# Six rounds of a local attention layer: a hardware loop over one body, or six bodies in sequence

## The chip, the cores and the metric

The kernel runs on one core of a Trainium2 chip (trn2). The metric is the device time of one execution in microseconds, as the median of several runs. Each core has five engines with instruction streams of their own: TensorE (PE), VectorE (DVE), ScalarE (ACT), GpSimd (POOL) and the sync engine (SP). They meet only at semaphores.

## What is computed

The reference is a network of four blocks on an activation of 4 x 512 tokens of 128 channels. Each block computes `x = x + s * silu(g)` from two sub-networks. The change is in the second sub-network of block 1, a transformer of six layers with attention in a window of 32 tokens:

```python
for i in range(6):
    x = attn_layer(shift_tokens(x), Wqkv[i], q_scale[i], k_scale[i], Wo[i]) + x
    x = ffn_layer(shift_tokens(x), ln_g[i], ln_b[i], W1[i], b1[i], W2[i], b2[i]) + x
```

`attn_layer` has 16 heads of 64: l2-normalised q and k, rotary factors, softmax over the token's own window of 32 and the one before, and the output product. `ffn_layer` is a layer norm, a gated product of 2 x 341 columns with an exact gelu, and the product back. All layers have the same shapes; only the weights differ. All data is float32.

## The kernel before

The activation lies in on-chip memory with channels on partitions and 2048 tokens along the free axis, in one of 20 slabs. The program is a sequence of phases. `phase` (lines 49 to 63) allocates semaphores, opens a block in which each engine gets its own list of instructions, and ends with clearing each semaphore (line 62, the clears dealt out to the five engines in turn) and an all-engine barrier (line 63). The block has a closing synchronisation of its own, which the profile puts down to line 58.

`local_transformer` (line 481) first has a phase that loads the attention weights of layer 0, the rotary tables and the masks, builds the shifted copy of the activation, and ends on VectorE with the product of tables and scales (line 518). Then it runs the layers as a hardware loop:

```python
with nc.Fori(0, F1_LAYERS) as layer:
    local_layer(nc, m, ins, layer, w, ...)
```

`local_layer` (line 536) is one phase with 48 semaphores. It has 32 units (16 tiles of 128 tokens, two halves of the heads), which pass through the engines as a pipeline written out by hand, unit i of one step beside units i-1 to i-6 of others (lines 747 to 799 on TensorE, 879 to 918 on ScalarE, 1019 to 1067 on VectorE, 1087 to 1091 on GpSimd). `project` (line 617) makes q and k of a unit with the products of line 623; a float32 product of 128x512 shows as two passes in the profile, so that a unit has four. `square` (line 807), `sum_squares` (937), `normalise` (949) and `rope` (1085, 957) follow. After the units the forward part runs in 12 chunks (lines 734, 735, 744). On the sync engine a round begins with the transfer of this layer's forward weights (`F1F`, line 598), goes on with the moves of the values, and ends with the transfer of the next layer's attention weights (`F1A`, line 612), which VectorE uses in line 1066. VectorE's last work in a round is `finish(3)`: the addition of line 1013 and two copies of line 1017. ScalarE begins a round with a table load (line 878) and has a second one in its middle (line 905).

After the layers comes a phase with one Silu on ScalarE (line 533), then the recurrent network, which has a hardware loop of its own with two rounds (line 1127) that stays as it is.

Of the kernel before, what the change touches and what calls it, by code (L numbers as in the profile page):

```python
# [26 lines left out]
def offsets(parts):  # L27

    at, where = 0, {}
    for name, width in parts:  # L30
        where[name] = (at, width)
        at += width
    return where, at
# [14 lines left out]
@contextmanager  # L48
def phase(nc, names, raised=False):

    with ExitStack() as ctx:
        sems = [ctx.enter_context(nc.semaphore(n)) for n in names.split()]
        if raised:
            for s in sems:
                nc.sync.sem_inc(s, RAISED)
            nc.all_engine_barrier()
        with nc.Block(no_gpsimd_drain=True) as block:  # L58
            yield (block, *sems)
        engines = [nc.sync, nc.tensor, nc.vector, nc.scalar, nc.gpsimd]  # L60
        for n, s in enumerate(sems):
            engines[n % len(engines)].sem_clear(s)
        nc.all_engine_barrier()  # L63
# [404 lines left out]
F1_LAYERS = 6  # L468
# [12 lines left out]
def local_transformer(nc, m, ins, xn, g_out):  # L481

    where, width = offsets(F1_ATTENTION + F1_FORWARD)
    W = m.slab(2, 3)[:, 0:width]
    for_attention = W[:, 0:offsets(F1_ATTENTION)[1]]
    for_forward = W[:, offsets(F1_ATTENTION)[1]:width]
    angles = m.slab(5)[:, 0:1024].rearrange("p (t k d) -> p t k d", t=4, k=4)
    tables = m.slab(5)[:, 1024:2048].rearrange("p (t k d) -> p t k d", t=4, k=4)
    shifted = m.slab(6, 2)[:, 0:BATCH * STRIP].rearrange("p (b t) -> p b t", b=BATCH)
    qBD = m.slab(7)[:, 256:1280].rearrange("p (n w h q) -> p n w h q", n=PAIRS, w=2, h=2)  # L490
    hA = m.slab(8, 2)[:, 0:BATCH * PADSEQ].rearrange("p (b t) -> p b t", b=BATCH)
    hB = m.slab(10, 2)[:, 0:BATCH * PADSEQ].rearrange("p (b t) -> p b t", b=BATCH)

    def w(name, a=0, n=None, rows=P):
        o, width = where[name]
        return W[0:rows, o + a:o + (a + n if n else width)]

    with phase(nc, "tables_loaded copied") as (block, tables_loaded, copied):
        @block.sync
        def _(sp):  # L500
            sp.dma_start(for_attention, ins["F1A"][F1_LAYERS - 1]).then_inc(tables_loaded, 16)
            sp.dma_start(m.slab(5)[:, 0:1024], ins["rotary"]).then_inc(tables_loaded, 16)
            sp.dma_start(m.masks[:, 0:2 * KEYS], ins["masks"]).then_inc(tables_loaded, 16)
            sp.wait_ge(tables_loaded, 48)

        @block.vector
        def _(dve):
            by_batch = xn.rearrange("p (b t) -> p b t", b=BATCH)
            nc.vector.memset(hB[:, :, 0:1], 0.0)
            nc.vector.memset(hA[:, :, 0:1], 0.0).then_inc(copied, 1)  # L510
            nc.vector.tensor_copy(hA[:, :, 1:PADSEQ], by_batch).then_inc(copied, 1)
            dve.wait_ge(copied, 2)
            for b in range(BATCH):
                for half, start in ((slice(0, 64), 1), (slice(64, P), 0)):
                    nc.vector.tensor_copy(shifted[half, b, REACH:STRIP], hA[half, b, start:start + SEQ])
            dve.wait_ge(tables_loaded, 48)
            by_side = w("scales").rearrange("p (o n) -> p o n", o=1).broadcast_to([P, 4, 4 * HD1])
            nc.vector.tensor_tensor(tables.rearrange("p t k d -> p t (k d)"), angles.rearrange("p t k d -> p t (k d)"), by_side, ALU.mult)

        @block.gpsimd  # L520
        def _(pool):
            nc.gpsimd.memset(m.weights[:, 0:2 * PAIRS * STRIP].rearrange("p (c t) -> p c t", c=2 * PAIRS)[:, :, 0:REACH], 0.0)
            nc.gpsimd.memset(shifted[:, :, 0:REACH], 0.0)
            nc.gpsimd.memset(m.slab(7)[:, 256:1280], 0.0)
            nc.gpsimd.memset(m.slab(16, 2), 0.0)

    with nc.Fori(0, F1_LAYERS) as layer:
        local_layer(nc, m, ins, layer, w, for_attention, for_forward, angles, tables, shifted, qBD, hA, hB)

    with phase(nc, "silu_done") as (block, silu_done):  # L530
        @block.scalar
        def _(act):
            nc.scalar.activation(g_out.rearrange("p (b t) -> p b t", b=BATCH), hA[:, :, 1:PADSEQ], ACT.Silu)

def local_layer(nc, m, ins, layer, w, for_attention, for_forward, angles, tables, shifted, qBD, hA, hB):
# [41 lines left out]
    def place(u):  # L578
        tile, half = u // 2, u % 2
        return tile // 4, tile % 4, half  # L580

    def moves(u):
        return 16 * sum(2 if place(n)[1] == 0 else 3 for n in range(u % 4, u + 1, 4))

    with phase(nc, "forward_loaded qk_product qT_product kT_product v_product score_product pT_product pv_product out_product "
# [9 lines left out]

        @block.sync
        def _(sp):
            sp.dma_start(for_forward, ins["F1F"][bass.ds(layer, 1)].rearrange("l p n -> (l p) n")).then_inc(forward_loaded, 16)
            for u in range(UNITS):
                b, t, half = place(u)  # L600
                sp.wait_ge(v_copied, u + 1)
                if u >= 4:
                    sp.wait_ge(pv_product, u - 3)
                sp.dma_start(v[u % 4][:, 1, :], tile_v[u % 4][REACH:P, :]).then_inc(moved[u % 4], 16)
                sp.dma_start(v[u % 4][REACH:KEYS, 0, :], tile_v[u % 4][0:WINDOW, :]).then_inc(moved[u % 4], 16)
                if t:
                    sp.dma_start(v[u % 4][0:REACH, 0, :], tile_v[(u - 2) % 4][P - REACH:P, :]).then_inc(moved[u % 4], 16)
            for n in range(4):
                sp.wait_ge(moved[n], moves(UNITS - 4 + n))
            sp.wait_ge(forward_loaded, 16)  # L610
            sp.wait_ge(out_product, UNITS // 2)
            sp.dma_start(for_attention, ins["F1A"][bass.ds(layer, 1)].rearrange("l p n -> (l p) n")).then_inc(next_loaded, 16)
            sp.wait_ge(next_loaded, 16)

        @block.tensor
# [1794 lines left out]
def block1(nc, m, ins, x):  # L2410
    xn = m.slab(1)
    spread_norm(nc, m, x, xn, tag="l1ln", refine=False)
    g, s = m.slab(2), m.slab(4)
    local_transformer(nc, m, ins, xn, g)
    recurrent_network(nc, m, ins, xn, s)
    add_product(nc, x, s, g)
# [220 lines left out]
```

## Time and profile before

| | us |
|---|---|
| median of 3 runs | 5192.08 |
| the runs | 5191.89, 5192.08, 5202.68 |
| the profiled execution | 5195.5 |
| its span, first to last instruction | 5193.7 |
| mean granted TensorE clock | 0.806 |
| busy: PE, DVE, ACT, POOL | 3971.8, 3768.7, 2570.9, 2171.7 |
| first round begins, last round ends (after the span's start) | 223.1, 2511.3 |

Times in rows are microseconds from the start of the span. In the timeline a row gives the start, the busy time of the merged instructions, the engine, the line, the operation, what it writes and reads with its shape, how many were merged, and in brackets how long the engine had been idle and what released it.
### The profile page before, as it was taken

What the parts mean: (1) busy time and instruction counts of PE and PEld (TensorE: products, weight loads), DVE (VectorE), ACT (ScalarE), POOL (GpSimd) and SP (SyncE); (2) the same over time, 40 slices, a digit from 0 to 9 for tenths busy, and PEclk for the clock granted to TensorE, in tenths of its full rate; (3) what the DMA queues carried; (4) which work ended last, traced back from release to release, by engine and by line L of the source; (5) the groups of instructions that cost most, each with busy time, mean ns of one, the idle gap of its engine ahead of it and who ended that gap; (6) DMA issues with size and microseconds to landing.
All of it is one profiled execution on the core that took longest, in us unless ns stands there. A gap on an engine that the chain in (4) does not pass through costs nothing. (4 is left out here: it accounts for less than half of the span.)

```text
span 5193.7 us, 75861 instructions
## 1 busy us (share of the span) xinstructions
PE 3971.8 (76%) x25476; PEld 2536.7 (49%) x25476; DVE 3768.7 (73%) x7356; ACT 2570.9 (50%) x6832; POOL 2171.7 (42%) x1600
## 2 busy tenths in 40 slices
PE   5389799799799799799777767956666666588897
PEld 2166466466466466466343343433333333355564
DVE  5799599599599598698354544399999999832343
ACT  2188488488488488488222121233333333326343
POOL 0177277277276376376120310066666666500000
PEclk8699899899899899899777687855555555567898
DMA  0011111111111111111000000000000000000000
GB/s 17 28 41 42 38 42 42 37 42 42 37 41 41 39 40 42 37 42 43 28 1 9 1 25 1 0 1 1 1 1 1 1 1 1 1 7 1 22 1 9
DMA packets 48634, 109.67 MB, mean 21 GB/s; under 512 B 8944, under 2 KB 9200, under 8 KB 46704
## 3 DMA queue, kind: packets, MB, share of 16 engines
q1 hardware_dynamic: 48240, 104.66, 6.6%
q8 instruction: 217, 3.56, 0.3%
q14 instruction: 177, 1.45, 0.1%
HBM read 31.23 MB, written 1.05 MB: 6 GB/s over the span
## 5 line engine op out<-in xcount | busy, mean ns | idle before, releaser
L1085 POOL TENSOR_TENSOR slabs<-slabs 128x512 f32<-128x512 f32 x768 | 975.4, 1300 | 368.7 <-DVE slabs L949 368.7
L1782 DVE MAX8 slabs<-slabs 128x8 f32<-128x512 f32 x1084 | 691.6, 679 | 57.4 <-ACT slabs L1719 57.4
L1808 POOL TENSOR_SCALAR slabs<-slabs 128x512 f32<-128x512 f32 x256 | 400.3, 1564 | 470.4 <-DVE slabs L1788 470.4
L1074 POOL TENSOR_TENSOR slabs<-slabs 128x768 f32<-128x768 f32 x192 | 341.9, 1781 | 567.9 <-DVE slabs L926 567.9
L623 PE MATMUL psum<-slabs 128*128 128x512 f32 x768 | 413.2, 665 | 214.7 <-DVE slabs L949 149.5
L1703 ACT ACTIVATE slabs<-slabs 128x512 f32<-128x512 f32 x316 | 211.6, 719 | 727.8 <-DVE slabs L1788 727.8
L854 ACT ACTIVATE slabs<-slabs 128x96 f32<-128x96 f32 x1536 | 551.4, 360 | 37.2 <-PE psum L667 35.7
L1641 PE MATMUL psum<-constants,slabs 128*128 128x128 f32 x1264 | 305.5, 407 | 299.7 <-POOL slabs L1811 299.3
L1784 DVE MATCH_REPLACE8 slabs<-slabs 128x512 f32<-128x512 f32 x768 | 513.0, 675 | 0.0
L1632 PE MATMUL psum<-slabs 8*128 8x512 f32 (+1 forms) x632 | 346.5, 1087 | 164.2 <-ACT slabs L1719 164.1
L659 PEld LDWEIGHTS psum<-weights,slabs 128*128 128x128 f32 x3072 | 372.2, 192 | 101.3 <-issue 86.1
L1641 PEld LDWEIGHTS psum<-constants,slabs 128*128 128x128 f32 x1264 | 222.6, 208 | 383.7 <-POOL slabs L1811 343.6
L957 DVE TENSOR_TENSOR slabs<-slabs 128x512 f32<-128x512 f32 x384 | 388.4, 1012 | 8.8 <-POOL slabs L1085 7.4
L659 PE MATMUL psum<-weights,slabs 128*128 128x96 f32 x3072 | 370.0, 274 | 8.8 <-ACT weights L826 8.8
L1811 POOL TENSOR_TENSOR slabs<-slabs 128x512 f32<-128x512 f32 x256 | 325.2, 1270 | 21.4
L623 PEld LDWEIGHTS psum<-slabs 128*128 128x128 f32 x768 | 141.2, 205 | 359.7 <-DVE slabs L949 185.3
L937 DVE TENSOR_REDUCE slabs<-slabs 128x16 f32<-128x1024 f32 x192 | 231.9, 1208 | 113.8 <-ACT slabs L807 112.9
L242 POOL TENSOR_TENSOR slabs<-slabs 128x512 f32<-128x512 f32 x12 | 17.4, 1484 | 671.2 <-POOLq L63 671.2
L854 ACT ACTIVATION_READ_ACCUMULATOR slabs<-slabs 128x1 f32 x1536 | 286.7, 187 | 0.0
L667 PE MATMUL psum<-constants,slabs 128*96 128x128 f32 x1536 | 244.9, 283 | 42.4 <-ACT slabs L847 39.2
L679 PEld LDWEIGHTS psum<-slabs 96*64 96x64 f32 x6144 | 195.7, 138 | 143.3 <-issue 134.8
L1632 PEld LDWEIGHTS psum<-slabs 8*128 8x128 f32 (+1 forms) x632 | 113.2, 294 | 300.9 <-ACT slabs L1719 281.4
(392 smaller groups left out, 8378.0 us busy)
## 6 DMA issues: line engine op xcount, KB each, us to landing
slabs<-slabs SPq DMA_DIRECT2D x192, 192.0 KB, 2.5
slabs<-slabs SPq DMA_DIRECT2D x192, 128.0 KB, 2.5
slabs<-F1A SPq DMA_DIRECT2D x7, 2176.0 KB, 8.4
slabs<-slabs SPq DMA_DIRECT2D x144, 64.0 KB, 2.1
slabs<-F1F SPq DMA_DIRECT2D x6, 580.5 KB, 4.2
slabs<-S SPq DMA_DIRECT2D x4, 645.0 KB, 6.5
weights<-M SPq DMA_DIRECT2D x1, 2184.0 KB, 9.4
weights<-R SPq DMA_DIRECT2D x2, 1079.5 KB, 5.5
```

The lines of the kernel that those rows point to most:

```text
L623: last = nc.tensor.matmul(ps[:, i, :], tokens, w(name, 512 * half, 512), start=True, stop=True)
L659: last = nc.tensor.matmul(SCORES[:, n // 4, n % 4, :], qBD[:, c, k, :, :], keys, start=True, stop=True)
L854: last = nc.scalar.activation(probs[:, n, :], masked[:, n, :], ACT.Exp, bias=shifts[:, n:n + 1], scale=8.0, accum_out=denom[:, n:n + 1])
L957: nc.vector.tensor_tensor(roped[:, at, :].rearrange("p h (s i) -> p h s i", s=2), cosines[:, at, :].rearrange("p h (s i) -> p h s i", s=2) ...
L1074: nc.gpsimd.tensor_tensor(probs, probs, scale, ALU.mult).then_inc(probs_ready, 1)
L1085: nc.gpsimd.tensor_tensor(out[:, at, :], normed[:, at, :], table, ALU.mult).then_inc(rope_done, 1)
L1632: nc.tensor.matmul(ps[:, j, :], q[rows, h // 4, b * SEQ + t * P:b * SEQ + t * P + P], keys[rows, h // 4, cols(b)], start=True, stop=True). ...
L1641: last = nc.tensor.transpose(ps[:, 4 + n % 2, k * P:k * P + P], probs[j][:, k * P:k * P + P], m.ident)
L1782: nc.vector.max(eight, work[side] if k else scores[slot + side]).then_inc(picked[b], 1)
L1784: nc.vector.match_replace(out=work[side], in_to_replace=eight, in_values=scores[slot + side] if k == 1 else work[side], imm_value=MASKED). ...
L1808: nc.gpsimd.tensor_scalar(kept[n % 2], scores[slot], tops[:, slot, TOPK - 1:TOPK], None, ALU.is_ge).then_inc(kept_ready, 1)
L1811: nc.gpsimd.tensor_tensor(probs[j], probs[j], kept[n % 2], ALU.mult).then_inc(probs_ready, 1)
```

## The change

The hardware loop becomes a loop of the program that writes the code. Each engine's stream then holds six bodies one after the other, with no counter and no branch back, and each body has its own phase, with the same semaphores to clear and the same barrier. `layer` is a constant, so the two transfers get constant addresses.

```diff
-    with nc.Fori(0, F1_LAYERS) as layer:
+    for layer in range(F1_LAYERS):
         local_layer(nc, m, ins, layer, w, for_attention, for_forward, angles, tables, shifted, qBD, hA, hB)
...
-            sp.dma_start(for_forward, ins["F1F"][bass.ds(layer, 1)].rearrange("l p n -> (l p) n")).then_inc(forward_loaded, 16)
+            sp.dma_start(for_forward, ins["F1F"][layer]).then_inc(forward_loaded, 16)
...
-            sp.dma_start(for_attention, ins["F1A"][bass.ds(layer, 1)].rearrange("l p n -> (l p) n")).then_inc(next_loaded, 16)
+            sp.dma_start(for_attention, ins["F1A"][layer]).then_inc(next_loaded, 16)
```

## Rows read from the trace of the kernel before

**Rows 1.** The page: the span and the instructions executed

```profile
span 5193.7 us, 75861 instructions
```

**Rows 2.** Timeline, end of round 1 and start of round 2: start us, us, what [idle before]

```profile
598.34 0.86 DVE L1017 COPY slabs<-slabs 64x512 f32<-64x512 f32 x2
601.68 0.35 SPq L598 DMA_DIRECT2D slabs<-F1F  x1
604.13 1.28 ACT L878 ACT_TABLE_LOAD   x1 [10.29 <-issue]
...
604.95 3.75 PE L623 MATMUL psum<-slabs 128*128 128x512 f32 x4 [7.43 <-issue]
```

**Rows 3.** The barrier's line L63 at the same place: start in us behind the comma

```profile
L63 PEldq EVENT_SEMAPHORE  x1: 51/51/51, 601.0 to 601.0; - x1
```

**Rows 4.** Timeline, the ends of rounds 2 to 5 and the next starts

```profile
980.68 0.86 DVE L1017 COPY slabs<-slabs 64x512 f32<-64x512 f32 x2
...
986.99 3.78 PE L623 MATMUL psum<-slabs 128*128 128x512 f32 x4 [7.13 <-issue]
...
1363.53 0.86 DVE L1017 COPY slabs<-slabs 64x512 f32<-64x512 f32 x2
...
1369.92 3.55 PE L623 MATMUL psum<-slabs 128*128 128x512 f32 x4 [7.21 <-issue]
...
1745.88 0.86 DVE L1017 COPY slabs<-slabs 64x512 f32<-64x512 f32 x2
...
1752.28 3.52 PE L623 MATMUL psum<-slabs 128*128 128x512 f32 x4 [7.22 <-issue]
...
2128.12 0.86 DVE L1017 COPY slabs<-slabs 64x512 f32<-64x512 f32 x2
...
2134.65 3.48 PE L623 MATMUL psum<-slabs 128*128 128x512 f32 x4 [7.36 <-issue]
```

**Rows 5.** Timeline, entry into the first round

```profile
220.95 1.22 DVE L518 TENSOR_TENSOR slabs<-slabs 128x1024 f32<-128x1024 f32 x1 [2.11 <-DMA window_masks<-masks]
223.01 1.28 ACT L878 ACT_TABLE_LOAD   x1 [28.01 <-PEq L63]
...
223.12 3.50 PE L623 MATMUL psum<-slabs 128*128 128x512 f32 x4 [28.85 <-PEq L63]
```

**Rows 6.** Timeline, the way out of the last round

```profile
2510.49 0.86 DVE L1017 COPY slabs<-slabs 64x512 f32<-64x512 f32 x2
2513.34 1.28 ACT L533 ACT_TABLE_LOAD   x1 [7.36 <-PEq L63]
```

**Rows 7.** DMA queues in 599:603.7, 223:600 and 605:982: packets, MB, share of 16 engines

```profile
q14 instruction: 3, 0.02, 2.0%
q8 instruction: 1, 0.02, 1.7%
...
q8 instruction: 21, 0.34, 0.4%
...
q8 instruction: 22, 0.36, 0.4%
```

**Rows 8.** Busy by stretch: us, PE, PEld, DVE, ACT, POOL, PEclk, DMA share, GB/s

```profile
598.43:601.84 3.41, 0.00 (x0) 0.00 (x0) 0.75 (x2) 0.00 (x0) 0.00 (x0) 0.98 0.01 2
601.84:605.25 3.41, 0.30 (x1) 0.30 (x2) 0.00 (x0) 1.12 (x1) 0.00 (x0) 0.50 0.63 186
```

**Rows 9.** Timeline, a later pair of the same products, inside round 1

```profile
304.07 1.98 PE L623 MATMUL psum<-slabs 128*128 128x512 f32 x4 [1.11 <-DVE slabs L949]
```

**Rows 10.** Lines L1066 and L612: durations in ns, first and last start in us

```profile
L1066 DVE TENSOR_TENSOR slabs<-slabs x6: 1209/1211/1211, 594.5 to 2506.7; 128x1024 f32<-128x1024 f32 x6
...
L612 SPq DMA_DIRECT2D slabs<-F1A x6: 346/347/351, 565.2 to 2477.3; - x6
```

**Rows 11.** DMA issues by tile: count, KB each, us to landing

```profile
slabs<-F1A SPq DMA_DIRECT2D x7, 2176.0 KB, 8.4
slabs<-F1F SPq DMA_DIRECT2D x6, 580.5 KB, 4.2
```

## The prediction

> **What bounds the kernel now.** I read the page first, for the span, 5193.7 us with 75861 instructions executed [rows 1]. The whole program is a string of phases with an all-engine barrier after each. The change touches only the six rounds of the local layer, so I went to the timeline at the joints of those rounds, because work inside a round stays instruction for instruction what it was. The reader is to see three things there.
>
> First, how long a joint lasts. Round 1 ends when VectorE's copy of L1017 ends, at 598.34 + 0.86 = 599.20; the first product of round 2 (L623) starts at 604.95 [rows 2]. Nothing computes in these 5.75 us. The four other joints read the same way [rows 4]: 981.54 to 986.99 (5.45), 1364.39 to 1369.92 (5.53), 1746.74 to 1752.28 (5.54), 2128.98 to 2134.65 (5.67). The five sum to 27.94 us, 5.59 each.
>
> Second, what the joint consists of. The barrier event of TensorE's queue is at 601.0, 1.8 us after the last work [rows 3]: this is the block's closing synchronisation, the clearing of some 48 semaphores spread over five engines, and the second barrier. From 601.0 to 604.95, 3.9 us, TensorE waits for nothing that the profile can name: its idle time is put down to "issue", where an engine waiting for a semaphore would have a releaser [rows 2]. ScalarE's table load at 604.13 also has "issue" as its cause. In that same stretch the instruction queues move packets, one on q8 and three on q14 [rows 7], while the sync engine is already issuing its transfer at 601.68. So the branch back to the top of the round leads to code that is not there, and each engine fetches it before it can go on.
>
> Third, what such a joint costs without a branch back. The entry into round 1 and the exit from round 6 are ordinary joints in sequence. At the entry DVE L518 ends at 222.17; ScalarE starts at 223.01 and TensorE at 223.12 [rows 5], 0.11 us later. That phase clears only two semaphores, so it is too short a model (0.95 us). At the exit L1017 ends at 2511.35 and ScalarE starts at 2513.34 [rows 6], 1.99 us, with the same semaphores to clear as in every round. Here the releaser is the barrier and not "issue".
>
> **The change part by part.** It removes the loop's register work and five taken branches, and lays six copies of the body one after the other on each engine.
>
> *The joints.* A joint in straight code is priced as the exit from round 6 plus TensorE's lag behind ScalarE at the entry: 1.99 + 0.11 = 2.10 us. Bounds from the nearest rows: 0.95 us (the entry) from below, 5.59 (nothing saved, the fetch still on the path) from above. I take 2.10, since its row has the same clears and the same two barriers. Saving: 5.59 - 2.10 = 3.49 us a joint, 5 x 3.49 = 17.4 us. After it the next thing late is TensorE's first product itself; ScalarE's table load (1.28 us) starts beside it and is over before the four passes of L623 (3.50 us, [rows 5]) are, so it remains covered.
>
> *The clock of the first product.* After each joint the four passes of L623 take 3.48 to 3.78 us [rows 2, 4]; inside a round, with the clock up, they take 1.98 [rows 9]. At the first joint the granted clock is still full in 598.43 to 601.84, though TensorE does nothing there, and at 0.50 (1.2 of 2.4 GHz) in the stretch after it [rows 8]. In straight code TensorE starts at 599.20 + 2.10 = 601.30, some 0.54 us before the clock fell. That is about one of the four passes at the full level, worth (3.50 - 1.98) / 4 = 0.4 us. Bounds: 0 if the clock falls before the start at every joint, and 5 x (3.75 - 1.98) = 8.9 us if it never falls. I take 0.4 x 5 = 2.0 us, as at the first joint, since nothing else in the rows tells me where the later ones would lie.
>
> *The code itself.* Six copies instead of one do not add fetches. q8 brings 21 packets in round 1, which is entered in sequence, and 22 in round 2, which is entered by the branch [rows 7]: each round fetches its whole code again as it is. In round 1 these 21 fetches stop nobody: its body, 223.12 to 599.20, takes 376.08 us, against 376.70 for round 6 (2134.65 to 2511.35) [rows 2, 4 to 6]. I cost fetching in sequence at 0; the cover is that the next block is asked for while the current one runs, and without it one stall costs what it costs at a joint, 5.59 - 2.10 = 3.5 us. On this the Trainium skill, in "Runtime: NRT & Kernel Launch", section "Instruction fetch mechanics", says that engines hold only a small part of a long program and stream the rest ahead of use, and that a taken branch to code outside what is held waits for a transfer. A looped body held resident would have made the joints free of fetches and this change worthless; by the page a body of this size cannot be, and the trace agrees, with 22 packets in round 2.
>
> *The two transfers with a layer index.* F1F at the start of a round (L598) and F1A at its end (L612) get a constant address. What goes is a register operation and a move on the sync engine for each. The number, size and order of the transfers stay, 580.5 KB and 2176 KB [rows 11]. F1A is issued at 565.2, lands in some 8.4 us, and its first user, L1066, starts at 594.5 [rows 10, 11]: 21 us of room. F1F is issued 0.4 us earlier after the barrier than now and is used only in the second half of the round. Both are worth 0. The sync engine has no other work queued behind them that anybody waits for at this time. No wait is added anywhere, and POOL's queue has the same instructions in the same order.
>
> *Loop entry and exit.* The entry costs no more than 0.95 us in all [rows 5] and at the exit the engines start on the barrier [rows 6], so I cost removing them at 0; the bound is a few tenths either way.
>
> **The sum.** 17.4 + 2.0 = 19.4 us. The profiled execution took 5195.5 us around its span of 5193.7, so it would take 5176.1. It lies 3.4 us above the median of the runs, 5192.08. Taken from the median: 5172.7, rounded 5173 us, 0.37% less.
>
> **The rivals.** The measurement of this kernel can tell about 0.2% from no change, 10.4 us: the three runs before span 5191.89 to 5202.68.
>
> (a) *The gain is partly given back later.* For it: TensorE's clock goes between its two levels in many places, and everything behind the first joint moves in time against those changes; code behind the layers also moves in its fetch blocks, and the recurrent loop behind it keeps its own branch back. The body times already differ from round to round, from 376.08 to 377.40 us (986.99 to 1364.39) [rows 2, 4 to 6]. Against it: that is 1.3 us at most in 380. If every one of the five later rounds came out at the worst body instead of 376.7, 5 x 0.7 = 3.5 us go; with as much again in the rest of the program twice over, some 10 us go in all, and the gain is 9 us: 5183.
>
> (b) *The clock stays up over the joint.* With the pause of TensorE about 3.5 us shorter, the clock may not fall at all at some joints. For it: it falls only late in the present pause [rows 8]. Against it: 3.8 us of the pause remain (TensorE's last product before it ends some 1.7 us before L1017 does), and the first three microseconds of idleness are in it either way. It gives up to 17.4 + 8.9 = 26.3 us: 5166.
>
> (c) *Slower: straight code is fetched just in time as well.* The place is the crossing from one fetched block to the next in rounds 2 to 6; the price is 3.5 us for each crossing at which TensorE arrives first. There are about 5 x 22 = 110 crossings. To end over 10.4 us slower it has to lose 10.4 + 19.4 = 29.8 us, 9 stalls out of 110; with 12 stalls it is 42 - 19.4 = 22.6 us slower, 5215. Against it: round 1 has the same 21 fetches in sequence and the shortest body of all [rows 2, 4 to 7].
>
> (d) *The change doesn't do what it says*: the joints remain at 5.6 us, because straight code too must fetch after a barrier. Then 5192. Against it: entry and exit show no fetch wait [rows 5, 6].
>
> **How the numbers follow.** The forecast has 0.64, (b) 0.12, (a) 0.16, (d) 0.05, (c) 0.03. The forecast itself spans 5168 to 5178 (the clock term from 0 to 4, the joint by half a microsecond each, and about 2 us of scatter). The range goes from 5164, below (b), to 5182, into (a), and leaves out the rest of (a), (c) and (d). Over 0.2% faster means under 5181.7: the forecast, (b) and a part of (a), 0.82. Within 0.2%: the rest of (a) and (d), 0.13. Slower: (c) and unknown effects of where the code lies, 0.05.
>
> **What would show it right or wrong.** Right: in the profile after, from the last end of L1017 in a round to the first L623 of the next there are about 2.1 us at all five joints, the table load of L878 names the barrier's L63 as its releaser and not "issue", and no q8 packet falls into that gap. The starts of successive rounds lie about 378.5 us apart instead of 382.2. The clock term is right if the first product at a joint takes 3.0 to 3.4 us. Wrong: joints of over 3 us with instruction packets in them (d); "issue" pauses of 3 us on TensorE inside a round (c); joints as forecast, but a part of the program behind 2514 us that is longer than before (a).

## The result and the profile after

The changed kernel takes 5157.23 us (median of 4 runs, 5151.78 to 5163.06), the kernel before, in the same measurement, 5193.40 (4 runs). The ratio is 0.9927, 95% interval 0.9910 to 0.9944. Two later measurements gave 0.9941 (0.9927 to 0.9954) and 0.9935 (0.9922 to 0.9949). The gain is 29 to 40 us where 19.4 were forecast; the time lies below the range.

The page of the changed kernel (against [rows 1]; q8 and q14 are the instruction queues, with packets and MB):

```profile
span 5150.0 us, 75756 instructions
...
PEclk8699899899899999999777688855555555567998
...
q8 instruction: 210, 3.44, 0.3%
q14 instruction: 173, 1.42, 0.1%
```

The span is 43.7 us shorter. The profiled execution took 5151.78 us, the lowest of its four, while that of before was 3.4 us above the median given with it, so this difference is larger than that of the medians. The timeline at three of the five joints (start us, us, what, idle time before with its releaser), against [rows 2, 4]:

```profile
596.98 0.86 DVE L1017 COPY slabs<-slabs 64x512 f32<-64x512 f32 x2
599.67 1.28 ACT L878 ACT_TABLE_LOAD   x1 [7.19 <-PEq L63]
599.68 0.34 SPq L598 DMA_DIRECT2D slabs<-F1F  x1
...
599.72 3.06 PE L623 MATMUL psum<-slabs 128*128 128x512 f32 x4 [3.56 <-PEq L63]
...
1351.93 0.85 DVE L1017 COPY slabs<-slabs 64x512 f32<-64x512 f32 x2
...
1354.83 3.62 PE L623 MATMUL psum<-slabs 128*128 128x512 f32 x4 [3.72 <-PEq L63]
...
1728.00 0.86 DVE L1017 COPY slabs<-slabs 64x512 f32<-64x512 f32 x2
...
1730.75 3.39 PE L623 MATMUL psum<-slabs 128*128 128x512 f32 x4 [3.57 <-PEq L63]
```

Round 1 ends at 596.98 + 0.86 = 597.84 and round 2 starts at 599.72: 1.88 us in place of 5.75. The releaser is now the barrier (PEq L63), not "issue". All five joints: 1.88, 1.87, 2.04, 1.89, 1.97, together 9.66 us in place of 27.96. DMA queues in round 1 of the changed kernel, 220.4 to 597.8, against [rows 7]:

```profile
q8 instruction: 22, 0.36, 0.4%
q14 instruction: 16, 0.13, 0.1%
```

In the joint itself, 597.8 to 600.0, neither queue has a packet. The number of fetches in a round has not changed: 21 or 22 on q8, as before.

Where did the 43.7 us go? I cut both traces at the barriers and at the last work of each round:

| part | before | after | difference |
|---|---|---|---|
| up to the first product of round 1 | 223.12 | 220.38 | -2.74 |
| six bodies | 2260.27 | 2253.19 | -7.08 |
| five joints | 27.96 | 9.66 | -18.30 |
| behind the last round | 2682.31 | 2666.78 | -15.53 |

The joints did what was forecast. The question for the experiments is the rest: the bodies, whose instructions are the same, and the part behind the layers, which the change does not touch.

### The profile page after: what moved, and what is told of

It reads as the page before. It is cut to its first block and busy times, and to the rows that moved or that the text cites. A ratio compares the mean times of both kernels' runs of the same rounds, so it can differ in the third digit from the quotient of the medians.

```text
span 5150.0 us, 75756 instructions
## 1 busy us (share of the span) xinstructions
PE 3947.6 (77%) x25476; PEld 2524.6 (49%) x25476; DVE 3769.9 (73%) x7356; ACT 2578.5 (50%) x6832; POOL 2173.6 (42%) x1600
## 5 line engine op out<-in xcount | busy, mean ns | idle before, releaser
L1074 POOL TENSOR_TENSOR slabs<-slabs 128x768 f32<-128x768 f32 x192 | 344.3, 1793 | 563.2 <-DVE slabs L926 563.2
L623 PE MATMUL psum<-slabs 128*128 128x512 f32 x768 | 408.9, 658 | 196.9 <-DVE slabs L949 151.4
L957 DVE TENSOR_TENSOR slabs<-slabs 128x512 f32<-128x512 f32 x384 | 384.8, 1002 | 7.8 <-POOL slabs L1085 7.4
L623 PEld LDWEIGHTS psum<-slabs 128*128 128x128 f32 x768 | 140.2, 203 | 339.9 <-DVE slabs L949 186.5
```

The source lines that it names most:

```text
L623: last = nc.tensor.matmul(ps[:, i, :], tokens, w(name, 512 * half, 512), start=True, stop=True)
L957: nc.vector.tensor_tensor(roped[:, at, :].rearrange("p h (s i) -> p h s i", s=2), cosines[:, at, :].rearrange("p h (s i) -> p h s i", s=2) ...
L1074: nc.gpsimd.tensor_tensor(probs, probs, scale, ALU.mult).then_inc(probs_ready, 1)
```

## The experiments

Three explanations stood first. S: the shortened rounds meet the changes of TensorE's clock differently. C: chance between executions. L: the code lies elsewhere in the blocks in which the engines fetch it. Each run stands beside the kernel before on the same chip, and the ratio is to that.

| run | median us (runs) | ratio, 95% interval | joints | bodies | of them 5th to last unit | behind |
|---|---|---|---|---|---|---|
| before, first profile | | | 27.96 | 2260.3 | 1526.3 | 2682.3 |
| before_again | 5194.20 (11) | 1.0010, 1.0001 to 1.0019 | 29.65 | 2262.8 | 1525.6 | 2681.6 |
| loop_shift | 5188.88 (11) | 0.9998, 0.9989 to 1.0007 | 29.00 | 2259.9 | 1526.5 | 2674.6 |
| loop_slot | 5172.72 (5) | 0.9962, 0.9948 to 0.9976 | 28.80 | 2252.2 | 1519.0 | 2674.1 |
| hint_loop | 5171.26 (5) | 0.9963, 0.9949 to 0.9976 | 12.87 | 2256.7 | 1525.5 | 2680.4 |
| hint_slot | 5165.37 (5) | 0.9954, 0.9940 to 0.9967 | 12.83 | 2258.6 | 1520.4 | 2671.5 |
| after, first profile | 5157.23 (4) | 0.9927, 0.9910 to 0.9944 | 9.66 | 2253.2 | 1521.7 | 2666.8 |
| after_again | 5160.06 (5) | 0.9941, 0.9927 to 0.9954 | 9.75 | 2252.0 | 1520.7 | 2673.7 |
| after_third | 5153.01 (5) | 0.9935, 0.9922 to 0.9949 | 9.66 | 2252.9 | 1519.4 | 2664.5 |
| straight_hit | 5166.92 (5) | 0.9952, 0.9939 to 0.9965 | 9.69 | 2257.7 | 1526.2 | 2674.7 |
| straight_miss | 5160.88 (6) | 0.9942, 0.9928 to 0.9955 | 9.58 | 2245.8 | 1517.0 | 2675.6 |
| straight_pause | 5186.57 (11) | 0.9993, 0.9984 to 1.0002 | 25.26 | 2256.5 | 1522.9 | 2672.8 |
| pause_half | 5175.40 (7) | 0.9965, 0.9954 to 0.9976 | 15.94 | 2256.6 | 1518.6 | 2678.1 |
| both_straight | 5166.15 (5) | 0.9941, 0.9928 to 0.9954 | 9.78 | 2255.6 | 1518.6 | 2678.2 |

The last four columns are sums over one profiled execution, in us; "5th to last unit" runs in each round from the end of the 5th normalising product (L949) to the end of the 32nd.

**before_again and after_again: how much is chance?** Both kernels unchanged.

> The kernel before once more, unchanged, for a second profile. Theory S (the extra gain outside the joints belongs to how the shortened program meets the changes of TensorE's clock): joints near 28 us in sum, bodies of the rounds 2258 to 2262 us in sum, the part behind the last round within 5 us of 2682. Theory C (chance between executions): the part behind the last round anywhere from 2665 to 2685, like that of any other execution.

> The changed kernel once more, unchanged. Joints 9.5 to 10.5 us in sum under every theory. Theory S: ratio near 0.993 again, bodies in sum 2250 to 2256 us. Theory C: the 36 us shrink towards the 18 us of the joints, ratio nearer to 0.996, and the part behind the last round is often near 2682 us instead of 2667.

Ratios 1.0010 and 0.9941. The body sums agree with the first profiles within 3 us, and before and after stay 7 to 11 us apart, so chance between executions does not explain that part. "Behind" differs by 7 us between two executions of the same changed program, so much of that part can be.

**hint_loop: the loop without its fetch.**

```diff
-    with nc.Fori(0, F1_LAYERS) as layer:
+    with nc.Fori(0, F1_LAYERS, hint_back_edge=True) as layer:
```

The timeline of hint_loop at the first joint (same columns):

```profile
602.40 0.86 DVE L1017 COPY slabs<-slabs 64x512 f32<-64x512 f32 x2
605.75 1.28 ACT L878 ACT_TABLE_LOAD   x1 [7.85 <-PEq L63]
...
605.89 3.77 PE L623 MATMUL psum<-slabs 128*128 128x512 f32 x4 [4.31 <-PEq L63]
```

**straight_pause: straight code, long joints.** Ahead of rounds 2 to 6 a phase of its own, which computes nothing that is needed:

```diff
+        if layer:
+            with phase(nc, "paused") as (block, paused):
+                @block.vector
+                def _(dve):
+                    nc.vector.memset(m.slab(17), 0.0).then_inc(paused, 1)
+                    dve.wait_ge(paused, 1)
```

> The changed kernel with a short phase of one VectorE fill of 128x2048 ahead of rounds 2 to 6, which computes nothing, so that each joint is about as long as it was in the loop (5 to 6 us) though nothing is fetched in it. S: time near that of the kernel before, 5180 to 5195, bodies in sum near 2260 us. L: only the length of the joints comes back, 5172 to 5178. C: about 5175 to 5190, with bodies of no fixed sum.

The timeline of straight_pause at the second joint (its lines are 7 higher than those of the kernel before, so L1024 is L1017 and L630 is L623):

```profile
978.39 0.86 DVE L1024 COPY slabs<-slabs 64x512 f32<-64x512 f32 x2
981.68 1.76 DVE L532 MEMSET slabs<- 128x2048 f32 x1 [2.44 <-PEq L63]
...
984.36 3.63 PE L630 MATMUL psum<-slabs 128*128 128x512 f32 x4 [6.79 <-PEq L63]
```

979.25 to 984.36 is 5.11 us; the five are 25.26 together. The time is close to that of the kernel before (ratio 0.9993), as S expected. But the bodies are not: 2256.5 and not near 2260. Neither theory is right as a whole. I laid the times between successive units side by side for all rounds, and there the cause of the bodies came out.

**What the bodies differ in.** In every round of the kernel before, eighteen of eighteen in three profiles, the step from the end of the 19th unit's L949 to that of the 20th takes 10.2 to 10.4 us; in the changed kernel it takes 9.2 to 9.3 in all eighteen. In round 2 of the kernel before that is 780.55 to 790.89, right behind the step in which the 15th unit's reciprocal runs, at 771.0; so I looked there for what was late. The timeline there, kernel before, round 2 (columns as above):

```profile
771.00 0.20 DVE L926 RECIPROCAL slabs<-slabs 128x8 f32<-128x8 f32 x1
...
771.28 1.47 POOL L1074 TENSOR_TENSOR slabs<-slabs 128x768 f32<-128x768 f32 x1 [2.74 <-DVE slabs L926]
...
771.43 1.87 DVE L957 TENSOR_TENSOR slabs<-slabs 128x512 f32<-128x512 f32 x1 [0.23 <-issue]
```

and the changed kernel at the same unit:

```profile
764.80 0.20 DVE L926 RECIPROCAL slabs<-slabs 128x8 f32<-128x8 f32 x1 [0.23 <-ACT slabs L854]
...
764.92 0.65 DVE L957 TENSOR_TENSOR slabs<-slabs 128x512 f32<-128x512 f32 x1
765.09 1.82 POOL L1074 TENSOR_TENSOR slabs<-slabs 128x768 f32<-128x768 f32 x1 [2.82 <-DVE slabs L926]
```

L957 follows L926 on VectorE and needs nothing new. In the changed kernel it starts at 764.92, before GpSimd's product L1074 (765.09), and takes 0.65 us. In the kernel before it starts 0.43 us after L926 did, with 0.23 us of idleness put down to "issue", after L1074 has begun, and takes 1.87 us. A pause of about 0.3 us has turned into a step over 1 us longer. The two instructions overlap in both kernels; what differs is which starts first. L957 stands directly behind L926 in 180 places of the program. In 174 of them, in the kernel before, it starts some 0.16 us ahead of L1074 and takes 0.65 us, and L1074 takes 1.8. In the six others L1074 starts 0.15 us ahead and takes 1.47 us, and L957 takes 1.87 and ends 0.55 us behind it. (Away from L926 an L957 over 1 us is common, 142 cases in the kernel before, and says nothing here; "the long L957" below is one directly behind L926.) The Trainium skill, "GPSIMD Engine Reference", section "Specifications", says that GpSimd's interfaces to SBUF are shared with VectorE, with contention where VectorE's instruction has two SBUF inputs; L957 is an addition of two slabs, and 1.87 against 0.65 us beside GpSimd's product agrees with it.

In the changed kernel this happens once in six rounds, in round 5, at the 13th unit, in all three of its profiles. That points to the cause of the pause: counted in VectorE's instructions in the trace (649 from barrier to barrier in a round of straight code), five pauses of 0.2 to 0.4 us stand out against the same instruction in the other rounds, and all their distances are multiples of 128. 649 is 5 x 128 + 9, so from round to round the pauses move 9 instructions forward in the body: from instruction 289 in round 1 to 289 - 36 = 253 in round 5, which is just behind L926 of the 13th unit. In the loop all rounds have them at the same instructions, one of them between L926 and L957. The instruction queue confirms it: 0.66 us behind the start of the late L957 a packet of q14 starts, at 389.76, 772.09, 1155.49 and 1536.85 us in the first four rounds of the kernel before, and in the changed kernel one starts 0.3 to 0.7 us behind each of the five pauses. I call this theory P; L is the same thought without the place.

**loop_shift: a run that moved nothing.**

```diff
+    for _ in range(12):
+        nc.vector.nop()
     with nc.Fori(0, F1_LAYERS) as layer:
```

> The loop of the kernel before, with 12 empty instructions on VectorE ahead of it (under 1 us), so that in every round VectorE crosses from one block of its code to the next 12 instructions earlier in the round. Theory P (place of the crossing): in the kernel before, the crossing falls in every round between the reciprocal of L926 and the addition of L957 of the 15th unit, VectorE starts L957 some 0.3 us late and meets GpSimd's product, and L957 takes 1.87 us instead of 0.65. With the shift no L957 behind L926 takes over 1 us, and from the fifth to the last unit a round takes 253.1 to 253.5 us instead of 254.2 to 254.4 (where no fall of the clock is in it); the time falls by 5 to 6 us, ratio 0.999. Theory S (only the clock and the length of the joints): that stretch stays at 254.2 or more and the time is the same, ratio 1.000. Joints stay at 5.5 to 6 us by both.

L957 remained long in all six rounds, and the ratio is 0.9998. Before this counts against P, look at the page's first line:

```profile
span 5183.9 us, 75861 instructions
```

It has as many instructions as the kernel before [rows 1]: the empty ones are not in the program that ran. The run is a third profile of the kernel before and no test.

**straight_hit and straight_miss: straight code, with the crossing put in place.** One line ahead of each round; the two differ in the offset, 96 and 108, alone:

```diff
     for layer in range(F1_LAYERS):
+        nc.engines[mybir.EngineType.DVE].addr_align(128, offset=96, max_nops=0)
```

> The changed kernel with VectorE's code of each round aligned so that the crossing falls, as in the loop, between L926 and L957 of the 15th unit in all six rounds. P: L957 takes 1.87 us in six places, the stretch from the fifth to the last unit 254.1 to 254.4 us in all six rounds without a fall of the clock; 5 to 6 us slower than straight_miss. S: the stretch stays at 253.1 to 253.5 and the two aligned kernels are the same.

> The same alignment with an offset greater by 12, so that the crossing falls 12 instructions earlier, where the shifted loop has it. P: no long L957, the stretch at 253.1 to 253.5 us, time within 5 us of the changed kernel (5155 to 5165). S: the same as straight_hit.

The timeline of straight_hit, round 2, 15th unit (lines are one higher):

```profile
767.58 0.20 DVE L927 RECIPROCAL slabs<-slabs 128x8 f32<-128x8 f32 x1 [0.16 <-ACT slabs L855]
...
767.87 1.47 POOL L1075 TENSOR_TENSOR slabs<-slabs 128x768 f32<-128x768 f32 x1 [2.75 <-DVE slabs L927]
...
768.03 1.85 DVE L958 TENSOR_TENSOR slabs<-slabs 128x512 f32<-128x512 f32 x1 [0.25 <-issue]
```

and of straight_miss:

```profile
765.57 0.20 DVE L927 RECIPROCAL slabs<-slabs 128x8 f32<-128x8 f32 x1 [0.15 <-ACT slabs L855]
...
765.69 0.65 DVE L958 TENSOR_TENSOR slabs<-slabs 128x512 f32<-128x512 f32 x1
765.85 1.82 POOL L1075 TENSOR_TENSOR slabs<-slabs 128x768 f32<-128x768 f32 x1 [2.75 <-DVE slabs L927]
```

straight_hit has the late and long addition in six rounds of six (1.85 to 1.87 us), straight_miss in none. From the fifth to the last unit the sums are 1526.2 and 1517.0 us, 9.2 apart; three rounds of straight_hit have a fall of the clock in this stretch, worth some 2.7 us together, and 6.5 us remain, 1.1 a round. The rounds without a fall take 253.8 to 254.1 and 252.7 to 252.9 us, each some 0.3 us less than expected. The medians differ by 6.0 us, in the forecast size, though the intervals of the two ratios overlap, so that the time alone would not prove it.

All 84 rounds of the 14 profiles agree. Of those without a fall of the clock in this stretch, the 21 with the long L957 take 253.8 to 254.4 us and the 42 without it 252.7 to 253.5.

**loop_slot: the loop, with the crossing moved.**

```diff
-    with nc.Fori(0, F1_LAYERS) as layer:
+    with nc.Fori(0, F1_LAYERS, head_slot={mybir.EngineType.DVE: 108}) as layer:
```

> The loop of the kernel before, with the head of VectorE's loop placed in its block of code as straight_miss has it (the 12 empty instructions of loop_shift are not in its program, so that run moved nothing and is only another profile of the kernel before). P: no L957 behind L926 over 1 us, the stretch from the fifth to the last unit 252.8 to 253.5 us in rounds without a fall of the clock, instead of 254.0 to 254.4; the time 5 to 8 us lower than before, ratio 0.9984 to 0.999. If the place of the crossing matters only in straight code, the ratio is 1.000 and the stretch stays. Joints 5.5 to 6 us.

The crossing has moved: in round 2 the last packets of q14 ahead of this L926 start at 766.64 and 769.48 us, and the next one comes after 780 us. The timeline of loop_slot, round 2, 15th unit:

```profile
774.69 0.20 DVE L926 RECIPROCAL slabs<-slabs 128x8 f32<-128x8 f32 x1 [0.17 <-ACT slabs L854]
...
774.81 0.65 DVE L957 TENSOR_TENSOR slabs<-slabs 128x512 f32<-128x512 f32 x1
774.97 1.82 POOL L1074 TENSOR_TENSOR slabs<-slabs 128x768 f32<-128x768 f32 x1 [2.77 <-DVE slabs L926]
```

No long L957 in the whole program, 1519.0 in place of about 1526 us from the fifth to the last unit, joints unchanged at 28.80. So P holds in the loop too, and no unrolling is needed to be rid of the long L957. The time fell by 17.7 us, more than the 5 to 8 expected and more than the 7 that this stretch shows. Its interval (0.9948 to 0.9976) ends at 12.5 us of gain, so some 5 us or more come with it that I can't put to a place.

**hint_slot: both on the loop.** The slot is 107, as the hint itself is one instruction.

```diff
-    with nc.Fori(0, F1_LAYERS) as layer:
+    with nc.Fori(0, F1_LAYERS, hint_back_edge=True, head_slot={mybir.EngineType.DVE: 107}) as layer:
```

> The same placement together with the prefetch hint of hint_loop. P: joints of 2.6 us as in hint_loop, no long L957, stretch 252.8 to 253.5; the two effects add up to 5.5 us times 3.2 less for the joints and 5 to 8 us for the crossing, ratio 0.9945 to 0.9965, at most 5 us from the changed kernel. If it stays at hint_loop's 0.9963 or above, the placement gives nothing on top.

5165.37 us, ratio 0.9954, joints 12.83, no long L957. That is within what was expected, but it does not show what the slot adds. hint_loop has no long L957 either: with the hint in the loop, the crossing at the 15th unit comes earlier. In round 2 the packet of q14 starts at 774.49 us, ahead of L926 (774.53), and L957 starts at 774.65 and takes 0.65 us. Its stretch sum of 1525.5 comes from four rounds with a fall of the clock; the two without take 253.4 and 253.5 us. So the hint shortens the joints and removes the long L957 too, the slot has none left to remove, and the intervals of hint_loop and hint_slot overlap. The gain of hint_slot is 25 us with a one-line edit of the loop, 10 us short of what the changed kernel shows on average (over its three measurements -36.2, -28.9 and -40.4 us).

**both_straight: the recurrent loop written out as well.**

```diff
-    with nc.Fori(0, 2) as layer:
-        load(nc, [(W, ins["R"][bass.ds(layer, 1)].rearrange("l p n -> (l p) n"))], "rwkv")
+    for layer in range(2):
+        load(nc, [(W, ins["R"][layer])], "rwkv")
```

> The changed kernel with the two rounds of the recurrent layers written out as well. If a branch back costs what the engines wait for code, the one joint there gets shorter by 0.5 to 1.5 us and nothing else changes: ratio to the kernel before 0.9935 to 0.9945, not to be told from the changed kernel. If the code's place behind the layers matters as it does within them, anything within 5 us of that either way.

0.9941, the same as after_again and straight_miss. TensorE's idle time ahead of the first product of the second recurrent round (L126) is 8.59 us where the three profiles of the changed kernel have 9.28 to 9.63, so that joint did get shorter; the time does not show it.

**pause_half and after_third: does the time follow the joints' length?** The fill of straight_pause cut to 256 columns, and the changed kernel beside it.

```diff
-                    nc.vector.memset(m.slab(17), 0.0).then_inc(paused, 1)
+                    nc.vector.memset(m.slab(17)[:, 0:256], 0.0).then_inc(paused, 1)
```

> straight_pause with a fill of 256 columns in place of 2048, so that the joints are about 3.5 us long instead of 5.05, or 1.93 in the changed kernel. If the time follows the length of the joints alone: 5 times 1.6 us more than the changed kernel of the same call, some 8 us, and 5 times 1.5 less than straight_pause. If the way in which the rounds meet the changes of TensorE's clock adds a part of its own that depends on the joints' length (straight_pause came out 26 us above the changed kernel where its joints are 16.6 us longer): more than 13 us or less than 3 us above the changed kernel.

> The changed kernel a third time, beside pause_half on the same chip and for a narrower ratio: 0.993 to 0.9945. Joints 9.6 to 9.8 us in sum, one long L957 (round 5, unit 13) in the whole program.

pause_half has joints of 15.94 us in sum, 6.3 more than after_third, and takes 22.4 us more, over the 13 that were the bound. So more came with the longer joints than their length. In straight_pause it is 26.5 us for 15.5, against after_again (the expectation has 16.6, with joints of 26.25 us in sum, 1 us too many). It isn't the long L957: neither kernel with a pause has one, and pause_half takes 1518.6 us from the fifth to the last unit. In the profiles of pause_half and after_third it is in the bodies (2256.6 against 2252.9) and most of it behind the rounds (2678.1 against 2664.5), where the programs do the same work. The pause also adds instructions and a barrier, which shift the code behind it, and no run tells that from the length of the joints.

**How the clock enters.** The forward part of a round (from the last L949 to the end) is the same work every time. Two successive rounds of loop_slot (columns: stretch, length, busy times with counts of PE, PEld, DVE, ACT and POOL, PEclk, DMA share, GB/s):

```profile
1284.67:1361.07 76.40, 66.08 (x439) 41.20 (x436) 38.34 (x80) 37.93 (x99) 11.92 (x8) 1.00 0.15 51
1663.46:1745.23 81.77, 72.81 (x439) 45.63 (x436) 38.24 (x81) 38.11 (x99) 11.92 (x8) 0.90 0.14 47
```

76.40 us with the clock up, 81.77 with more of it at half. Over the 84 rounds of all profiles the length of this part follows the time at the lower level: 76.4 us with none (4 rounds), 76.6 to 77.2 with 3.4 us of it (16), 77.5 to 78.5 with 6.8 (37), 78.7 to 79.9 with 10.2 (16), 80.2 to 80.3 with 13.7 (7), 81.8 with 17.1 (4). The kernels before and after have the same mean here, 78.4 and 78.2.

Behind the rounds the largest single difference is the phase that starts at 3180.5 us in the kernel before. Before, after, and after_again:

```profile
3180.50:3313.20 132.70, 130.21 (x256) 45.18 (x256) 43.98 (x64) 22.46 (x37) 0.00 (x0) 0.94 0.00 0
```

```profile
3146.50:3273.60 127.10, 124.55 (x256) 43.42 (x256) 43.98 (x64) 22.48 (x37) 0.00 (x0) 0.98 0.00 0
```

```profile
3150.30:3282.90 132.60, 130.07 (x256) 45.08 (x256) 43.98 (x64) 22.45 (x37) 0.00 (x0) 0.94 0.00 1
```

The same 256 passes and 64 VectorE instructions take 132.7, 127.1 and 132.6 us. In the first and in the third profile of the changed kernel this phase and the two ahead of it run faster together (184.5 in place of 195 us; the phase behind gives back 2.2), in the second one, as in all three profiles of the kernel before, they don't. The 14 runs of the changed kernel fall into two groups, six from 5151.7 to 5153.7 and eight from 5156.6 to 5166.2; the profiles of 5151.8 and 5153.0 us are those with the fast phases, that of 5160.1 is not. That the runs of 5151.8 to 5153.7 us without a profile have the fast phases too is not shown. Why the changed kernel meets them and the one before did not in three profiles is open: the work in these phases is the same, and no run sets the time at which they begin by itself.

## Why the prediction was wrong

The time of 5157 us lies under the range of 5164 to 5182, and the gain is about twice the forecast in the first measurement and 1.5 and 2.1 times in the other two. By its own steps:

*The joints* were right, in mechanism and size. 2.10 us were forecast for each and 1.93 measured; 17.4 us of saving against 18.30 in the profile. The sums, on average of three profiles of either kernel, are 28.9 and 9.7, a difference of 19.2 us. The price from the exit of round 6 [rows 6] held, the cause was the fetch behind the branch back [rows 2, 7], and hint_loop shows it from the other side: with the code asked for in time the loop's joints fall to 2.57 us. Rounds start 377.8 us apart, where the prediction had 378.5 (382.3 before; it wrote 382.2).

*The clock of the first product* was the right mechanism and too large. 0.4 us a joint were forecast. The four passes of L623 took 3.06, 3.75, 3.62, 3.39 and 3.57 us, 17.39 in sum against 18.08 before: 0.7 us in place of 2.0, and 1.3 on average of three profiles each (17.2 and 18.5). The clock fell up to 0.7 us before the first product at four of the five joints, and only the first joint shows most of a pass at full speed; the prediction took that one as the model of all five.

*The code itself* is the first step that failed. I costed fetching in sequence at 0, on the ground that round 1 has 21 fetches and the shortest body, and I went only to the joints, "because work inside a round stays instruction for instruction what it was". The instructions stay, but their place in the fetched blocks does not. In the loop every round has its pauses at the same instructions, round 1 too, so comparing round 1 with the other rounds could not show it. One of them cost 1.1 us a round. Straight code spreads them over the body and hits such a pair of L926 and L957 once in six rounds. Measured: 1526.1 us from the fifth to the last unit on average of three profiles before, 1520.6 after, 5.5 us. The row was there to be read: behind L926 the addition takes 1.87 us at the 15th unit of each round and 0.65 us everywhere else, with "issue" in front of the long one. This step alone would not have broken the range: 19.4 + 5.5 = 24.9 us gives 5167, inside it.

*The part behind the rounds* is the second step that failed, and the larger one. The sum has it at 0, the gain side of the range has no room for it, and rival (a) lets it only lose. It came out 11.2 us shorter on average of three profiles each (2679.5 and 2668.3), with executions of one program up to 9 us apart. The largest term in it is the attention phase at the higher clock with the phases beside it, some 8 us, in two of three profiles. What made the changed kernel meet the higher clock there stays open.

*The rivals.* (a), given back later, didn't come. (b), the clock up over the joints, would have given the nearest number but didn't happen: 0.7 us. (c), stalls in sequence, is refuted as a loss, and yet its mechanism is real: pauses at crossings exist, in the loop and in straight code, of 0.2 to 0.4 us where it had 3.5. (d) is refuted by the joints.

On average of three profiles each, the 38 us are 19.2 for the joints, 5.5 for the crossing, 2.8 for the rest of the bodies (1.3 of it the first products) and 11.2 behind, with -0.5 ahead of round 1. The crossing is shown by runs that change it alone, in straight code (straight_hit, straight_miss) and in the loop (loop_slot). The joints are read from the traces, and that their cost was the fetch is shown by hint_loop, though its hint moved the crossing as well. What of the last ones is systematic is open: loop_slot gained 17.7 us with 7 accounted for, and the two pauses lost 11 to 16 us more than their length.

## What to carry to other kernels

Price a hardware loop's round by reading one joint inside it and one at its exit: with "issue" as releaser and instruction packets in the gap, the branch back is on the path, and a prefetch hint gets most of it without writing the loop out. Then compare successive repetitions inside the body: a step that is long in every round at the same place, with "issue" ahead of it, can come from where the code lies, and here moving the loop's head by 12 instructions on one engine removed it. An edit that adds a single instruction to the loop, as the hint does, moves this place too, so look at it again before a gain is put down to the edit. Where TensorE's clock goes between its levels, leave 5 to 10 us in 5000 on the gain's side of the range as well, for any change that moves the timing.

## What the runs showed of the hardware

- A joint with a branch back and instruction packets in it cost 3.3 to 4.2 us more than the same joint in straight code (5.39 to 6.08 against 1.87 to 2.06); a hint at the head of the round leaves 2.53 to 2.63.
- VectorE's pauses for 0.2 to 0.4 us lie at distances of multiples of 128 instructions in straight code, and at the same instructions in every round of a loop. The Trainium skill, "Runtime: NRT & Kernel Launch", section "Instruction fetch mechanics", has blocks of 256 instructions whose crossing is mostly hidden. Here q14, whose packets start 0.3 to 0.7 us behind VectorE's pauses, moves 0.13 MB in 16 packets a round, 8 KB each, where those of q8 have 16 KB (0.36 MB in 22). The pause is short but not hidden.
- Such a pause of 0.3 us cost 1.1 us a round, where it let GpSimd start first: 1.87 us for an addition that otherwise takes 0.65. With VectorE first by 0.16 us the addition is not drawn out and GpSimd's product takes 1.8 us in place of 1.47.
- The same attention phase takes 127.1, 129.5 to 129.7, or 132.6 to 133.1 us in the 14 profiles; PEclk is 0.98 in the first and 0.94 in the last case.
